# A fused four-block transformer kernel: a 128-point Hadamard product moved ahead of the butterfly in the last block, and a reordered prelude

## The reference

```
def fwht(x):           # normalized Walsh-Hadamard transform of the last axis
def act_quant(x):      # per token: scale = 127/max|x|, round, unscale
def h_bitlinear(x, w): # act_quant(fwht(x)) times ternary(w)
gate = h_bitlinear(hidden, w_gate)      # 512 -> 2048
up   = h_bitlinear(hidden, w_up)
return h_bitlinear(silu(gate) * up, w_down)   # fwht over 2048 values, then 2048 -> 512
```

## Time and profile before

| | |
|---|---|
| median of 3 runs | 804.4 us (803.64 to 804.83) |
| profiled execution | 803.61 us, span of its instructions 801.8 us |
| granted TensorE clock, mean | 0.982 |
| busy, whole span | PE 730.3, DVE 609.0, ACT 420.8, POOL 261.5 us |
| prelude to the first gate_up_b | 45.9 us |
| block d | from 487 us |

### The profile page before, as it was taken

How to read it: one execution, slowest core, us unless ns; L and a number is a source line. 1 busy time by engine, 2 the same in 40 slices (tenths; PEclk the granted TensorE clock), 3 DMA queues, 4 the chain that set the end, 5 groups by cost and what they waited for, 6 DMA issues and landing times. The chain is left out here.

```text
span 801.8 us, 13264 instructions
## 1 busy us (share of the span) xinstructions
PE 730.3 (91%) x4443; PEld 448.9 (56%) x4480; DVE 609.0 (76%) x1308; ACT 420.8 (52%) x931; POOL 261.5 (33%) x164
## 2 busy tenths in 40 slices
PE   1579999999999999989999999669999999999947
PEld 0266767666767675844444444345565665655644
DVE  6777987887887685457887856987888888887864
ACT  3645676566656463422212124347776676777545
POOL 3000000000000000010000001697887888888740
PEclk9989999999999999999999999989999999999969
DMA  8960141112111214722324100000000000000001
GB/s 194 264 235 1 41 132 40 41 40 80 40 40 48 72 40 143 278 105 66 145 105 144 66 1 0 1 1 14 14 14 14 13 27 13 13 13 13 15 13 40
DMA packets 24646, 51.71 MB, mean 64 GB/s; under 512 B 2066, under 2 KB 4114, under 8 KB 23572
## 3 DMA queue, kind: packets, MB, share of 16 engines
q1 hardware_dynamic: 21684, 45.96, 16.9%
q0 software_dynamic: 2480, 4.33, 3.0%
q10 hardware_dynamic: 432, 0.79, 0.3%
HBM read 51.20 MB, written 4.19 MB: 69 GB/s over the span
## 5 line engine op out<-in xcount | busy, mean ns | idle before, releaser
L1348 PE MATMUL ps<-arena 128*128 128x256 f16 x1408 | 163.9, 275 | 5.9 <-DVE arena L928 3.0
L1348 PEld LDWEIGHTS ps<-arena 128*128 128x128 f16 x1408 | 136.5, 98 | 33.6 <-DVE arena L928 9.7
L1471 PE MATMUL ps<-arena 128*128 128x512 bf16 x484 | 117.3, 379 | 5.2 <-DVE arena L1124 3.6
L406 POOL TENSOR_TENSOR arena<-arena 128x1024 f32<-128x1024 f32 x42 | 101.4, 2415 | 41.4 <-DVE arena L1133 38.2
L1305 PE MATMUL ps<-I,arena 128*128 128x128 f32 x576 | 82.7, 286 | 29.9 <-ACT arena L481 13.1
L407 POOL TENSOR_TENSOR arena<-arena 128x1024 f32<-128x1024 f32 x42 | 101.2, 2409 | 0.0
L354 POOL TENSOR_TENSOR rstd_a<-ve_a,mhalf 128x1 f32<-128x1 f32 x32 | 19.5, 611 | 249.7 <-DVE ve_a L779 243.3
L1305 PEld LDWEIGHTS ps<-I,arena 128*128 128x128 f32 x576 | 70.3, 147 | 53.3 <-issue 22.1
L507 ACT ACTIVATE arena<-ps,gs 128x256 f32<-128x256 f32 x88 | 41.1, 467 | 78.5 <-PE ps L1348 78.5
L354 POOL TENSOR_TENSOR rstd_b<-ve_b,mhalf 128x1 f32<-128x1 f32 x32 | 17.6, 551 | 192.2 <-DVE ve_b L779 192.2
L1359 PE MATMUL ps<-arena 128*128 128x512 f16 x352 | 78.6, 379 | 0.0
(11 more groups left out here) (129 smaller groups left out, 1184.5 us busy)
## 6 DMA issues: line engine op xcount, KB each, us to landing
arena<-in_ctx_t SPq DMA_DIRECT2D x7, 1024.0 KB, 5.3
arena<-in_wg_t SPq DMA_DIRECT2D x16, 256.0 KB, 3.4
arena<-in_wu_t SPq DMA_DIRECT2D x16, 256.0 KB, 3.9
arena<-in_wd_t SPq DMA_DIRECT2D x16, 256.0 KB, 4.1
arena<-in_ctx_n SPq DMA_DIRECT2D x4, 1024.0 KB, 7.5
arena<-in_wg_t SPq DMA_DIRECT2D x4, 1024.0 KB, 4.9
arena<-in_wu_t SPq DMA_DIRECT2D x4, 1024.0 KB, 4.7
arena<-in_wd_t SPq DMA_DIRECT2D x4, 1024.0 KB, 5.3
```

The lines of the kernel that those rows point to most:

```text
L406: nc.gpsimd.tensor_tensor(b[:, :, 0, :], a[:, :, 0, :], a[:, :, 1, :], ALU.add).then_inc(d_bfp, 1)
L1348: last = M(bank(n % 2)[:, 2 * P * i:2 * P * i + 2 * P], W[:, b, c * P:c * P + P], part[:, b, at:at + 2 * P], start=(b == 0 and part is xhT ...
L1471: last = M(bank(2 * (n % 2) + i), d_qT[u][:, b, :], W[:, b, D * n:D * n + D], start=(b == 0), stop=(b == KD - 1))
```

## The change

- **Order of the transform in block d.** `h_turn` now transposes the hidden values HA themselves; the 128-point product (`h_product`, before `h_last_bits`) comes next, for tile k-1 instead of k-2. The butterfly between blocks follows it: ScalarE copies the odd 128-blocks of each product bank to HB (`odd_evac`, 256 values for each of four banks), VectorE's `first_stage` reads the even blocks from PSUM and the odd from HB (eight operations of 256 values for each tile), and GpSimd does the other three stages (HB, HC, HD, Y). `back_max` reads Y in two pieces of 1024 instead of four of 512. `y_evac` is gone.
- **Orders.** Each engine's body k is reordered; `d_fill` and both shared butterflies of tile 0 are gone, so bodies 0 to 15 all use the general body (first bodies written out by the same function). `down` is split into 11 and 5 matmuls around `h_product` 0 and 1. `d_norm(k + 2)` is VectorE's last operation of the body.
- **Last tile.** TensorE does 9 of its 11 factors with the full 512-point matrix (`last_product`, 32 matmuls of 512 columns); VectorE does the remaining two (`last_stages`). GpSimd's third stage of tile 14 goes to VectorE (`late_stage`).
- **Prelude.** All four context bands are rounded by VectorE; `first_context_rounding` on GpSimd is gone; maxima before the second tile's statistics; `a_product(0)` before `a_turn(1)`; `b_norm(0)` before `a_residual(1)`; GpSimd issues the weight DMAs before the second `root`; the identity in fp16 is made later; the first `gate_up_b` takes the eight high-half products first.

VectorE, prelude:

```diff
             a_stats(0)
+            for b in range(KD):
+                first_context_max(b)
             a_stats(1)
-            for b in (3, 0, 1, 2):
-                first_context_max(b)
```

VectorE, block d; between the two parts of body k stand `d_hidden` 0, `h_rest(k - 1)` 0 and 1, `d_hidden` 1, `front_scales`, `d_hidden` 2, `stats`, `d_hidden` 3, `h_rest` 2 and 3:

```diff
-            def first_stage(j, u):
...
-                a, b = (t.rearrange("p (a t w) -> p a t w", t=2, w=P) for t in (HA[u], HB))
-                V.tensor_tensor(b[:, :, 0, :], a[:, :, 0, :], a[:, :, 1, :], ALU.add).then_inc(d_bf0, 1)
-                V.tensor_tensor(b[:, :, 1, :], a[:, :, 0, :], a[:, :, 1, :], ALU.subtract).then_inc(d_bf0, 1)
+            def first_stage(j, n):
+
+                dve.wait_ge(d_Y_r, 4 * j + n + 1)
+                a, b = (t.rearrange("p (a t w) -> p a t w", t=2, w=P) for t in (bank(6 + n % 2), HB[:, D * n:D * n + D]))
+                V.tensor_tensor(b[:, :, 0, :], a[:, :, 0, :], b[:, :, 1, :], ALU.add)
+                V.tensor_tensor(b[:, :, 1, :], a[:, :, 0, :], b[:, :, 1, :], ALU.subtract).then_inc(d_bf0, 1)
...
+                if on(k - 2):
+                    first_stage(k - 2, 2)
+                    first_stage(k - 2, 3)
                 if out_part:
-                    back_max(k - 3, w, 2)
-                    back_max(k - 3, w, 3)
+                    back_max(k - 3, w, 0)
+                if front and not at(k, 0):
+                    d_low(k + 1)
+                if out_part:
+                    back_max(k - 3, w, 1)
                     back_scales(k - 3, w)
...
+                if back:
+                    first_stage(k - 1, 0)
+                    first_stage(k - 1, 1)
                 if out_part:
                     d_residual(k - 3, w)
...
+                if ahead:
+                    d_norm(k + 2, u)
```

GpSimd, body k:

```diff
+                if on(k - 2):
+                    pool_stage(k - 2, 0)
+                    pool_stage(k - 2, 1)
+                if on(k + 2):
+                    root("d", k + 2, u)
+                if on(k - 2) and not at(k, NT):
+                    pool_stage(k - 2, 2)
```

ScalarE, whose body k is now `odd_evac(k - 2)` 2 and 3, `d_high(k + 1)`, `d_silu` 0, `h_evac(k - 1)` 0 and 1, `d_silu` 1, `y_round(k - 3)`, `d_silu` 2, `yq_evac(k - 3)`, `d_round(k + 1)`, `d_silu` 3, `h_evac` 2 and 3, `d_turned(k + 1)`, `odd_evac(k - 1)` 0 and 1:

```diff
+            def odd_evac(j, n):
+
+                act.wait_ge(d_y, 4 * j + n + 1)
+                if n == 0:
+                    wait(act, d_bfp, 6 * j - 4)
+                a, b = (t.rearrange("p (a t w) -> p a t w", t=2, w=P) for t in (bank(6 + n % 2), HB[:, D * n:D * n + D]))
+                nc.scalar.activation(b[:, :, 1, :], a[:, :, 1, :], ACT.Copy).then_inc(d_Y_r, 1)
```

TensorE, whose body k is now `gate_up` 0, `d_turn(k + 1)`, `h_turn(k - 1)` 0 and 1, `gate_up` 1, `d_front(k + 1)`, `gate_up` 2, `yq_turn(k - 3)`, `gate_up` 3, `h_turn` 2 and 3, `q_turn(k + 1)`, `down(k - 3, 0, 11)`, `h_product(k - 1)` 0 and 1, `down(k - 3, 11)`, `h_product` 2 and 3:

```diff
+            def h_product(j, n):
+                if n == 0:
+                    pe.wait_ge(d_hl_r, 4 * j + 4)
                 if n >= 2:
...
+                    pe.wait_ge(d_bf0, 4 * j + n - 1)
...
             def d_drain():
...
+                    last_product(n)
+                for j in (13, 14, 15):
+                    yq_turn(j)
+                    down(j)
```

More of the change, by code:

```diff
@@ L701, in d_body @@
                     yq_evac(k - 3, 1)
-                if mid:
+                if front:
+                    d_round(k + 1, w)
+                if mid and out_part:
+                    d_silu(k, u, 3)
+                if back:
+                    h_evac(k - 1, 2)
+                    h_evac(k - 1, 3)
+                if mid and not out_part:
                     d_silu(k, u, 3)
@@ L1226, in d_body @@
-                if at(k, 2):
-                    d_norm(5, 1)
-                elif on(k + 2) and not early:
-                    d_norm(k + 2, u)
-                if back:
-                    back_max(k - 2, u, 0)
-                    back_max(k - 2, u, 1)
+                if back:
+                    h_rest(k - 1, 2)
+                    h_rest(k - 1, 3)
+                if mid and not out_part:
+                    d_hidden(k, u, 3)
+                if back:
+                    first_stage(k - 1, 0)
+                    first_stage(k - 1, 1)
@@ L1271, in d_drain @@
+            def d_drain():
+                first_stage(14, 2)
+                first_stage(14, 3)
+                for n in range(4):
+                    h_rest(15, n)
                 back_max(13, 1, 0)
                 back_max(13, 1, 1)
-                last_add(2)
-                back_max(13, 1, 2)
-                back_max(13, 1, 3)
                 back_scales(13, 1)
-                last_add(3)
-                for n in range(4):
-                    h_rest(14, n)
-                d_residual(12, 0)
@@ L1281, in d_drain @@
-                for n in range(4):
-                    h_rest(15, n)
-                for n in range(4):
-                    back_max(14, 0, n)
+                last_stages(0)
+                late_stage()
+                back_max(14, 0, 0)
+                back_max(14, 0, 1)
                 back_scales(14, 0)
+                last_stages(1)
                 d_residual(13, 1)
-                for n in range(4):
-                    back_max(15, 1, n)
+                back_max(15, 1, 0)
+                back_max(15, 1, 1)
@@ L1553, in down @@
                     pe.wait_ge(d_add, j - 1)
-                for c in range(C1):
+                for c in range(first, end):
                     if c % 8 == 0:
@@ L1580, in d_body @@
                 if out_part:
-                    pe.wait_ge(d_hl_r, 4 * j + 8)
-                    yq_turn(j)
-                if mid:
+                    yq_turn(k - 3)
+                if mid and out_part:
+                    gate_up(k, u, 3)
+                if back:
+                    h_turn(k - 1, w, 2)
+                    h_turn(k - 1, w, 3)
+                if mid and not out_part:
                     gate_up(k, u, 3)
```

493 lines of the change are left out of this document (146 added, 347 removed).

## The result

The median of five runs is 780.18 us (779.2 to 781.26), before 804.46; the ratio is 0.9698, 95% interval [0.9683, 0.9712]. That is 24.3 us less, where 17.7 were forecast. The sign, the likeliest case and its order were right; 780.2 lies inside the range, 6.8 under the predicted 787.0.

What follows compares the result with a forecast made beforehand. TensorE was full in blocks b and c, so only the two ends and block d could move. Bodies 2, fill 5.8, drain 3.4 and prelude 6.5 sum to 17.7 us less: 785.9 profiled, median 787 us, own range 779 to 793.

Steps and rivals of the forecast that it cites:

- the body is 17.41, not 18.2: First rival, chance 0.20: VectorE becomes the steady bound, a body takes 18.2 to 18.5 us; time 795.
- block b started at 39.96, not 43: Second rival, chance 0.10: late DMA of weights or last context band hides the prelude's gain, block b near 43; 791.
- Prelude, -6.5 forecast: Before block b: a_product 0 no longer waits for a_turn 1, first gate-up at 39.2; 6.5 us less, bounds 4 and 8.
- Fill, -5.8 forecast: Block d's first bodies, run through the general body: body 4 starts at 545.5 against 551.3; 5.8 us less, bounds 3 and 8.
- The walk: Fill and drain: following the new order operation by operation with priced durations, giving 5.8 and, before the clock allowance, 5.4 less.
- Steady bodies, -2 forecast: Bodies 4 to 14 of block d: 17.55 us each, bounds 17.3 and 18.3; 11 bodies x 0.2 = 2 us less.
- (1): Steady bodies, TensorE alone: 17.3 us, with h_product 2 just fitting and 3 late by 0.1 to 0.2.
- (2): Steady bodies, ring through VectorE, from d_hidden 0 round to d_hidden: 17.1 us.
- (3): Steady bodies, ring through GpSimd: six operations and a root, 14.9, then d_norm and first_stage 2 and 3: 17.0 us.
- The collision rival: Third rival, chance 0.04: d_norm meets a GpSimd operation in every steady body, a body takes 19.6; 809.
- Drain, -3.4 forecast: From gate_up(15, 0) to the end: 55.2 us becomes 49.8, less a clock allowance; 3.4 us less, bounds 7 and -1.
- the allowance for the clock: Drain: 2 us added for part of one down at half speed, since TensorE mostly waits from 31 to 36.6 and 40 to 43.

Runs made afterwards that it cites:

- h3: Kernel after plus 7 unused float32 matmuls of 512 columns behind the row of down scales in the prelude; 780.19 us, 0.9702 of the kernel before.
- w1: Kernel after with the five down matmuls between h_product 1 and 2 moved ahead of h_product 0; 794.78 us, 0.9884 of the kernel before.
- g1: Kernel after plus one unused GpSimd operation of 1024 values in each tile's second stage; 794.96 us, 0.9891 of the kernel before.
- q1: Kernel after plus unused matmuls: 7 behind the down-scales row, 3 between the b_turns, 3 between down 13 and yq_turn 14; 778.5 us, 0.9688 of before.
- z1: Kernel after, but ScalarE copies all 512 columns to SBUF and first_stage reads both inputs there; 798.32 us, 0.9927 of the kernel before.
- h2: Kernel after plus unused matmuls: 14 behind the down-scales row, 5 between the b_turns, 1 behind them; 783.82 us, 0.9759 of the kernel before.
- h4: Kernel after plus unused matmuls: 7 behind the down-scales row and 3 between the b_turns; 778.62 us, 0.9679 of the kernel before.
- h1: Kernel after plus 14 unused float32 matmuls of 512 columns behind the down-scales row; 782.12 us, 0.9735 of the kernel before.

## Why the prediction was right, and what was mis-sized

**Which case.** The change gained in all four places that the prediction named, by the mechanisms that it named as far as runs and traces show them. No rival came: the body is 17.41, not 18.2; block b started at 39.96, not 43; no norm in the steady bodies took more than 0.55 us.

**Prelude, -6.5 forecast, -6.0 at block b and -6.2 at block d.** `context_top` (9.96, forecast 9.9) and product 0's start (23.76, forecast 24.4) were right. Product 0 ended near 30.5 in place of 29.5, since I let it end with `context_back` 3, and its 8 passes alone took 6.7 us at 0.85 each. h3 shows that it was this and not ScalarE: the faster passes ended at 27.5. Block b's start was again at the low clock, as I allowed. The seven kernels with this prelude start block b 6.0 to 7.2 us before the kernel before, so the 6.5 lies in their midst, and part of the closeness is luck: product 0's clock was a term that the sum did not have.

**Fill, -5.8 forecast, -6.8 measured.** The walk's milestones, shifted by the 6.2 us of the prelude, against the starts in the trace:

| gate_up 0 of tile | 1 | 2 | 3 | 4 |
|---|---|---|---|---|
| forecast | 490.8 | 505.4 | 520.6 | 539.3 |
| measured | 490.83 | 505.34 | 520.50 | 538.28 |

The stalls of bodies 1 and 2 came where they were put, and smaller in the first (TensorE's timeline):

```profile
502.39 1.07 PE L1387 MATMUL ps<-H,arena 128*128 128x128 f16 x16 [0.34 <-DVE arena L1092]
504.28 1.28 PE L1387 MATMUL ps<-H,arena 128*128 128x128 f16 x16 [0.82 <-DVE arena L1040]
```

The norm's collision in body 2 came too (1.88 us at 519.95). The us that was missed lies in body 3, where I had put 1.5 us of stalls and TensorE was busy 19.68 of the 20 us from 520 to 540. A second thing I had not read in the earlier trace rows: the 3.59 us of `d_front` at 536.33 before are at half clock (the granted clock was 0.50 from 534.8 to 541.6), twice the 1.9 that it takes elsewhere. Without the 5.28 us of waiting before it, that went too. It was in the time before, so it did not spoil the sum.

**Steady bodies, -2 forecast, -3.6 measured.** 17.55 was a guess between 17.3 and 18.3 for three rings that "will rub". The rings are there, and what was mis-sized is the rubbing. (1) is as computed: TensorE is busy for 17.26 of the 17.41, with short waits of 0.26 and w1 for its cover. The prices of (2) came, 0.42 and 0.33, and its waits are 8 of 0.3. (3) has the right mechanism, as g1 shows, and was drawn 0.6 too long: 16.4 in place of 17.0. GpSimd's turn takes 14.6, not 14.9, and between two turns lie 1.77 us, not 2.1, since a norm that meets the last operation ends 0.28 behind it. So (3) had 1.0 us of room and not 0.4, no norm met GpSimd, and TensorE all but alone set the body.

The collision rival rested on a real ring. Its price was too high: 1.3 a body in g1's last eight, not 2.05. The argument against it, that the ring is self-limiting, did not hold: in g1 the later norm did make GpSimd start later, and the two still met in every one of the eight bodies. (The body from which that rival decides is 17.55 + 17.7 / 11 = 19.2, not the 19.4 of the text, which adds to the old body what is counted from the new one.)

**Drain, -3.4 forecast, -6.8 measured: the mis-sized term.** From gate_up 0 of tile 15 (729.80 after) the walk and the trace, us:

| | forecast | measured |
|---|---|---|
| last_product ends | 25.4 | 25.1 |
| GpSimd's two stages of tile 14 end | 27.4 | 26.8 |
| late_stage ends | 30.2 | 29.3 |
| scales of 14 end | 33.4 | 32.3 |
| last_stages 1 and residual 13 end | 36.5 | 35.2 |
| scales of 15 end | 39.7 | 38.3 |
| end | 49.8 | 48.6 |

1.2 us come from a walk a little slow in each VectorE step, 2.0 are the allowance for the clock, and 0.2 the start that I read for the drain before (746.6, a weight load at 746.39). The clock did fall behind the longest hole, as feared, but for 3.4 us (before: 13.6, from 766.9 to 780.5). One `down` shows it, 4.45 in place of 3.40; the last `down` ran at 3.40. q1 and the six drains beside it put the price at 0.2 to 0.6. So of the 2 us some 1.4 to 1.8 were too much, and the walk, which had none of that price, was slow by 1.4 to 1.8. The allowance came from a reading of the earlier trace rows that took the old drain's 0.84 as what would stay, though the longest stall in it, the 8.13 us of waiting, was what the change removed.

Sum of the misses: 0.3 (prelude) - 1.0 (fill) - 1.6 (bodies) - 3.4 (drain) = -5.7, and -0.9 from the medians against the profiled executions: 6.6 of the 6.8; the rest is rounding.

## What to carry to other kernels

Walk the new order through the fill and the drain with the durations of the trace: both walks came within 1.2 us of 49 and 58, while the allowance put on top of the drain's was 1.4 to 1.8 too much. The idle time of an engine is not the room of a ring through it: part of it is the ring itself. Measure the room where the two engines would meet, and test it with two dummy operations, one shorter and one longer than the distance; and look at the bodies one by one, since an average over two regimes hides the ring. One profiled execution is no baseline for a gain of a microsecond: kernels with the same prelude started block b up to 1.2 us apart. And moving one operand of a VectorE operation from SBUF to PSUM can be worth more than the bytes: here 0.8 us a body beside a busy GpSimd.

## What the runs showed of the hardware

- A `tensor_scalar` of VectorE that met a GpSimd operation ended 0.28 us after it: 1.88 us in place of 0.54 in the kernel after (519.95), 1.9 to 2.6 in g1. It waited for that one operation and not for the next: at 538.86 in g1 it took 0.70 while GpSimd's next operation had begun. A two-input addition in SBUF did the same, 1.28 in place of 0.41 (z1).
- The stretch of low clock around the start of block b lasted 3.4 us in five kernels and 6.8 us in two with the same prelude and the same holes of 8.9 and 2.8 us in front of it. Filling the second hole removed it in all three kernels that did so (h2, h4, q1); filling the first alone did not (h1: 3.4 us, h3: 6.8). What decides between 3.4 and 6.8 is open: no run varied it alone.
- The profile's clock column showed 1.00 up to 29.9 us in the kernel after, where float32 passes started 0.85 apart; in h3 they started 0.43 apart. The kept trace has no clock record before 29.87 us, so for that stretch the spacing of the passes tells the level, and the column does not.
